# Attention by transposed scores in a fused convolution, attention and step-network kernel

## The reference

```
x = x + depthwise_conv_51x51(group_norm(x))
t = tokens(x)                                # (16, 256, 32)
h = layer_norm(t)
t = t + softmax(mask(Q K^T / sqrt(32))) V Wo + bo   # mask: window, stride, spikes of a sequential gate
h = layer_norm(t)
for p in 33 steps:                           # step network
    op = argmax(h[0, 0, :19])
    if attn_mask[p][op]: h = softmax(h wq wk^T h^T / sqrt(32)) h wv wo
    if ffn_mask[p][op]:  h = relu(h w1 + b1) w2 + b2
t = t + h
```

## Time and profile before

| | us |
|---|---|
| median of 3 runs | 200.5 (199.66 to 201.96) |
| span of the profiled execution | 199.1 |
| TensorE busy | 166.5 |
| VectorE busy | 134.3 |
| ScalarE busy | 111.3 |
| GpSimd busy | 64.1 |

### The profile page before, as it was taken

One profiled execution on the slowest core, in us unless ns is written; L12 is line 12 of the kernel. 1 busy time (PEld: TensorE's weight loads), 2 busy tenths in 40 slices (PEclk: granted clock), 3 DMA queues, 4 the chain that ended last, 5 costly groups with the idle time before them and its releaser, 6 DMA issues.

```text
span 199.1 us, 4262 instructions
## 1 busy us (share of the span) xinstructions
PE 166.5 (84%) x1255; PEld 112.6 (57%) x1256; DVE 134.3 (67%) x382; ACT 111.3 (56%) x324; POOL 64.1 (32%) x153
## 2 busy tenths in 40 slices
PE   7999989693898998879929679999867699998770
PEld 5779744241685776647412468776533587775320
DVE  1364578819938889896506388898756689789481
ACT  3464511429767656555405568675655877664670
POOL 8940000100061555453600005655510036556300
PEclk9999999969579999999966999999999999999997
DMA  5900000000000000000000100000000000000003
GB/s 158 315 3 0 3 0 3 0 3 2 0 2 0 2 0 3 0 0 18 3 7 2 20 0 0 0 0 0 0 0 15 0 0 0 0 0 0 0 0 110
DMA packets 3020, 3.33 MB, mean 17 GB/s; under 512 B 889, under 2 KB 2361, under 8 KB 3002
## 3 DMA queue, kind: packets, MB, share of 16 engines
q1 hardware_dynamic: 2858, 2.85, 4.8%
q10 hardware_dynamic: 144, 0.25, 0.4%
HBM read 2.58 MB, written 0.53 MB: 16 GB/s over the span
## 4 chain that ended last, share of the span: by engine, by line
PE 60%; DVE 16%; issue 9%; ACT 8%; POOL 2%; DVEq 1%; ACTq 1%; POOLq 0%
PE bank L555 17%; PE bank L528 8%; PE bank L615 5%; PE bank L542 5%; ACT qz L981 4%; PE bank L679 4%; PE bank L813 3%; PE bank L512 3%; DVE big L1269 3%; PE bank L633 3%; PE bank L600 2%; POOL prob L448 2%; PE bank L694 2%; ACT qz L1050 1%; ACT prob L905 1%
## 5 line engine op out<-in xcount | busy, mean ns | idle before, releaser
L448 POOL TENSOR_SCALAR prob<-prob,einv 128x256 f32<-128x256 f32 x96 | 44.7, 478 | 60.6 <-DVE einv L1264 60.4
L1269 DVE COPY big<-bank 128x512 f32<-128x512 f32 x48 | 32.9, 685 | 5.7 <-PE bank L528 5.7
L905 ACT ACTIVATE prob<-bank,nmax 128x256 f32<-128x256 f32 x64 | 29.8, 473 | 11.6 <-DVE nmax L1256 11.6
L528 PE MATMUL bank<-ident,prob 128*128 128x128 f32 x192 | 30.2, 280 | 6.5 <-POOL prob L448 6.4
L555 PE MATMUL bank<-hT,qz 128*128 128x256 f32 x128 | 32.7, 383 | 0.0
L528 PEld LDWEIGHTS bank<-ident,prob 128*128 128x128 f32 x192 | 21.4, 140 | 18.2 <-POOL prob L448 14.1
L1256 DVE TENSOR_REDUCE nmax<-bank 128x2 f32<-128x512 f32 x32 | 21.6, 687 | 4.8 <-PE bank L555 4.6
L555 PEld LDWEIGHTS bank<-hT,qz 128*128 128x128 f32 x128 | 22.3, 190 | 3.6 <-issue 1.6
L905 ACT ACTIVATE prob<-minus,nmax 128x256 f32<-128x256 f32 x32 | 16.0, 500 | 8.9 <-DVE nmax L1253 7.9
L555 PE MATMUL bank<-kt,qz 128*128 128x256 f32 x64 | 16.5, 386 | 0.9 <-ACT prob L905 0.9
L905 ACT ACTIVATION_READ_ACCUMULATOR prob<-bank,nmax 128x1 f32 x64 | 12.9, 202 | 0.0
(11 more groups left out here) (173 smaller groups left out, 256.8 us busy)
## 6 DMA issues: line engine op xcount, KB each, us to landing
xrev<-xrev_dram SPq DMA_DIRECT2D x1, 512.0 KB, 4.5
xin<-xtok_dram SPq DMA_DIRECT2D x1, 512.0 KB, 5.0
out_dram<-outT SPq DMA_DIRECT2D x2, 256.0 KB, 3.3
maskc<-maskc_dram SPq DMA_DIRECT2D x1, 256.0 KB, 4.8
kx<-kx_dram ACTq DMA_DIRECT2D x1, 248.0 KB, 3.1
wx<-wx_dram SPq DMA_DIRECT2D x1, 216.0 KB, 2.9
constf<-constf_dram SPq DMA_DIRECT2D x1, 186.0 KB, 4.6
wa<-wa_dram SPq DMA_DIRECT2D x3, 56.0 KB, 1.8
```

What stands on the lines that cost most here:

```text
L448: last = nc.gpsimd.tensor_scalar(prob[b % NPB][:, ih, :], prob[b % NPB][:, ih, :], einv[:, b, ih:ih + 1], 1.0, ALU.mult, ALU.mult)
L528: mm = pe.transpose(bank[2 + b % 2][:, jh * S + ih * P:jh * S + (ih + 1) * P], prob[b % NPB][:, ih, jh * P:(jh + 1) * P], ident)
L905: e = nc.scalar.activation(prob[b % NPB][:, ih, :], scores, ACT.Exp, bias=nmax[:, b, ih:ih + 1], scale=-1.0 if masked else 1.0, accum_out= ...
L1269: nc.vector.tensor_copy(flat(probT[b % NTB]), bank[2 + b % 2][:, :]).then_inc(s_PT, 1)
```

## The change

The product of the attention is turned over. It does the following.

- Queries are drained whole into `qT` (one instruction a group, all on ScalarE), without zeros. `score_pe` multiplies in one row strip of 32 partitions; batch elements 2n and 2n+1 use two strips, and the shifted scores of the pair three rounds earlier use the other two, in turn of h, so that four strips can run side by side.
- The maxima come from these scores (`row_max` as before). GpSimd splits each into three bf16 parts (`parts`, four small instructions for a pair), TensorE turns them to rows (`max_rows_pe`), ScalarE copies the rows to SBUF, and `shift_pe` adds them, by a bf16 product with ones, to every row of a bank; in the masked attention the transposed mask enters by one more bf16 product of 128 rows and 512 columns. `shifted_pe` adds the transposed scores K Q^T onto that.
- ScalarE does one exponential of 512 columns for an element, straight into `probT`. Scaling of `prob`, transposes and `copy_probT` are gone.
- `weigh_pe` also forms the sums of exponentials: a product with ones over `halves`, which GpSimd adds from the two halves of `probT` for elements 0 to 11; for the last group over `probT` itself. `normed_output` on VectorE inverts them (128x256) and multiplies. One bank (6) holds the output of every group.
- The masked attention's residual adds go to GpSimd for groups 0 and 1. A `halves` buffer, the transposed mask (`maskt`, one more load of the size of `maskc`) and a bf16 identity are new. The memset of `qz` on GpSimd is replaced by smaller ones.
- In the loop's body the block of kind 1 stands first, `kind` is computed again, and the attention of the next step follows in the same pass. In the block of kind 3 the products with w2 for groups 0 and 1 are ahead of the second `hidden`. The table load that `nc.scalar.activation(table, Exp)` brings stands once ahead of the loop, not in each attention.

The core of the diff ("..." marks what is left out):

```diff
+        RING = 2
+        NPAIR = B // 2
+        LAG = 3
+        FIRST = 2 * LAG
+        SBANK = [b if b < FIRST else b % 3 for b in range(B)]
+        TBANKS = [3 + b % 3 for b in range(B)]
+        YBANK, MBANK = 6, 7
...
+        ATTY = "DDDD"
+        LPRE = "AAAA" + "AAAA"
...
+        def attention_pool(pool, base, masked):
+            for n in range(NPAIR + 2):
+                if n < NPAIR:
+                    bs = slice(2 * n, 2 * n + 2)
+                    top2 = nmax[:, bs, :].rearrange("p b h -> p h b")
+                    rest2 = rest[:, bs, :].rearrange("p b h -> p h b")
+                    wait(pool, s_nm, base, 2 * n + 2)
+                    nc.gpsimd.tensor_copy(parts[:, :, bs, 0], top2).then_inc(s_hi, 2)
+                    wait(pool, s_hi, base, 2 * n + 2)
+                    nc.gpsimd.tensor_tensor(rest2, top2, parts[:, :, bs, 0], ALU.subtract)
+                    nc.gpsimd.tensor_tensor(parts[:, :, bs, 1], top2, parts[:, :, bs, 0], ALU.subtract).then_inc(s_mid, 2)
+                    wait(pool, s_mid, base, 2 * n + 2)
+                    nc.gpsimd.tensor_tensor(parts[:, :, bs, 2], rest2, parts[:, :, bs, 1], ALU.subtract).then_inc(s_part, 2)
+                if n >= LAG + 1:
+                    for b in (2 * (n - LAG - 1), 2 * (n - LAG - 1) + 1):
+                        if b < B - GB:
+                            wait(pool, s_P, base, b + 1)
+                            nc.gpsimd.tensor_tensor(halves[:, b, :], probT[b][:, 0, :], probT[b][:, 1, :],
+                                                    ALU.add).then_inc(s_ps, 1 if b < B - GB - 1 else 1 + GB)
+                if masked and n >= NPAIR:
+                    masked(n - NPAIR)
...
-        def turn_pe(pe, base, b):
-            wait(pe, s_Pn, base, b + 1)
-            if b >= 2:
-                wait(pe, s_PT, base, b - 1)
-            for jh in range(NH):
-                for ih in range(NH):
-                    mm = pe.transpose(bank[2 + b % 2][:, jh * S + ih * P:jh * S + (ih + 1) * P],
-                                      prob[b % NPB][:, ih, jh * P:(jh + 1) * P], ident)
-            mm.then_inc(s_T, 1)
...
+        def score_pe(pe, b, h, keys):
+            g, rows, at_row = strip(b)
+            mm = pe.matmul(bank[SBANK[b]][:, h * S:(h + 1) * S], qT[rows, g, h * P:(h + 1) * P], keys[rows, g, :],
+                           start=True, stop=True, tile_position=at_row)
+            if h == NH - 1:
+                mm.then_inc(s_S, 1)
+        def shifted_pe(pe, b, h, keys):
+            g, rows, at_row = strip(b)
+            mm = pe.matmul(bank[TBANKS[b]][:, h * S:(h + 1) * S], keys[rows, g, h * P:(h + 1) * P], qT[rows, g, :],
+                           start=False, stop=(h == NH - 1), tile_position=at_row)
+            if h == NH - 1:
+                mm.then_inc(s_T, 1)
...
+        def max_rows_pe(pe, base, n):
+            wait(pe, s_part, base, 2 * n + 2)
+            to = slice(2 * C * (n % 2), 2 * C * (n % 2 + 1))
+            if n >= 2:
+                wait(pe, s_mr, base, 2 * n - 2)
+            for h in range(NH):
+                mm = pe.matmul(bank[MBANK][to, h * P:(h + 1) * P], flat(parts[:, h, 2 * n:2 * n + 2, :]), identb[:, :],
+                               start=True, stop=True, tile_position=(0, 2 * C * (n % 2)))
+            mm.then_inc(s_M, 2)
+        def shift_pe(pe, base, n, masked):
+            wait(pe, s_mr, base, 2 * n + 2)
+            for b in (2 * n, 2 * n + 1):
+                if b >= FIRST - 3:
+                    wait(pe, s_P, base, b - 2)
+                else:
+                    wait(pe, s_nm, base, b + 4)
+                g, rows, at_row = strip(b)
+                if masked:
+                    pe.matmul(bank[TBANKS[b]][:, :], identb[:, :], flat(negmT[:, :, :]), start=True, stop=False)
+                pe.matmul(bank[TBANKS[b]][:, :].rearrange("p (h s) -> p h s", h=NH), onesq[rows, :], rep(mrow[rows, g, :], NH),
+                          start=not masked, stop=False, tile_position=at_row)
...
         def weigh_pe(pe, base, t, k0, g):
+            t.drained(pe, k0 + g)
+            if t is st and g == 0:
+                pe.wait_ge(s_vb, NG * NH)
+            wait(pe, s_P, base, GB * (g + 1))
+            out = bank[YBANK]
             for jh in range(NH):
                 for q in range(GB):
                     b = g * GB + q
+                    pe.matmul(out[q * C:(q + 1) * C, 0:S], v[:, jh, b, :], probT[b][:, jh, :],
+                              start=(jh == 0), stop=(jh == NH - 1), tile_position=(0, q * C))
+            if t is st:
+                pe.matmul(out[:, S:2 * S], onesq[0:1, :], tiny[:, :], start=True, stop=False)
+            if g < NG - 1:
+                wait(pe, s_ps, base, GB * (g + 1) if g < NG - 2 else B)
+                for q in range(GB):
+                    mm = pe.matmul(out[q * C:(q + 1) * C, S:2 * S], onesc[:, :], halves[:, g * GB + q, :],
+                                   start=t is not st, stop=True, tile_position=(0, q * C))
+            else:
+                for jh in range(NH):
+                    for q in range(GB):
+                        mm = pe.matmul(out[q * C:(q + 1) * C, S:2 * S], onesc[:, :], probT[g * GB + q][:, jh, :],
+                                       start=t is not st and jh == 0, stop=(jh == NH - 1), tile_position=(0, q * C))
             mm.then_inc(s_task, 1)
...
+            for h in range(NH):
+                for b in bs:
+                    score_pe(pe, b, h, keys)
+        def attention_pe(pe, base, t, k0, keys, ahead, masked=None):
+            ahead()
+            t.drained(pe, k0)
+            max_rows_pe(pe, base, 0)
+            for n in range(LAG, NPAIR + LAG):
+                if n - LAG + 1 < NPAIR:
+                    max_rows_pe(pe, base, n - LAG + 1)
+                shift_pe(pe, base, n - LAG, masked)
+                if n < NPAIR:
+                    wait(pe, s_nm, base, 2 * n - 1 if n > LAG else 2)
                 for h in range(NH):
+                    for i in range(2):
+                        if n < NPAIR:
+                            score_pe(pe, 2 * n + i, h, keys)
+                    for i in range(2):
+                        shifted_pe(pe, 2 * (n - LAG) + i, h, keys)
+                if n >= LAG + 2 and n % 2 == 1 and n < NPAIR + LAG - 1:
+                    weigh_pe(pe, base, t, k0, (n - LAG - 2) // 2)
+                if masked and n == NPAIR + 1:
+                    masked()
...
+                    wait(pe, s_P, att, B - 2)
+                    t.drained(pe, K_HF - 1)
+                    token0(r)
+                    hidden(r, 0)
+                    token0_row()
+                    weigh_pe(pe, att, t, len(LPRE), NG - 1)
+                    k = K_HF + GB + 1
+                    t.drained(pe, k - 1)
+                    outputs(t, k, (0, 1))
+                    t.drained(pe, k)
+                    hidden(r, 1)
                     next_step(pe, b, reg_r, reg_op, reg_code)
-                    for n in range(NG):
-                        if n % 2 == 0:
-                            t.drained(pe, k0 + GB if n == 0 else k1 + GB)
-                        for q in range(GB):
-                            mm = pe.matmul(bank[ZBANK[n]][q * C:(q + 1) * C, 0:S], w2s, relu[:, q, n, :],
-                                           start=True, stop=True, tile_position=(0, q * C))
-                        mm.then_inc(s_task, 1)
+                    t.drained(pe, k + 2 + GB)
+                    outputs(t, k + 2 + GB, (2, 3))
...
+            copy_rows(0)
+            for n in range(NPAIR):
+                if n + 1 < NPAIR:
+                    copy_rows(n + 1)
+                for b in (2 * n, 2 * n + 1):
+                    wait(act, s_T, base, b + 1)
+                    nc.scalar.activation(flat(probT[b]), bank[TBANKS[b]][:, :], ACT.Exp).then_inc(s_P, 1)
...
+            def normed_output(t, k, g, to):
+                t.filled(dve, k)
+                link(nc.vector.reciprocal(sinv[:, g, :], bank[YBANK][:, S:2 * S]))
+                return nc.vector.tensor_tensor(to[:, g, :], bank[YBANK][:, 0:S], sinv[:, g, :], ALU.mult)
...
+            def attention_dve(base, masked, output, late=None):
+                for b in range(B):
                     row_max(base, b, masked)
+                    if b == B - 3:
+                        output(0)
+                    if late and b >= B - 2 - GB and b < B - 2:
+                        late(b - (B - 2 - GB))
+                output(1)
```

More of the change, by code:

```diff
@@ new lines, in hidden, with outputs @@
+                def hidden(r, gp):
+                    for q in range(GB):
+                        rows = slice(q * C, (q + 1) * C)
+                        if (gp, q) == (1, GB - 1):
+                            pe.wait_ge(s_rowc, r)
+                        pe.matmul(bank[HBANK[gp][q]][:, :], w1r[rows, :], flat(hT[rows, 2 * gp:2 * gp + 2, :]),
+                                  start=True, stop=True, tile_position=(q * C, 0)).then_inc(s_task, 1)
```

(44 more changed lines are left out.)

519 lines of the change are left out of this document (224 added, 295 removed).

## The result

The changed kernel takes 238.2 us (median of 4 runs, 236.3 to 243.0) against 201.1 beside it (199.7 to 202.0): ratio 1.182, interval 1.172 to 1.192. The direction was right, the size was not: 37 us longer where the forecast had 23, and 2 us outside its range. The profiled execution is the slowest of the four, 243.0 us with a span of 241.2; the others had spans of 234.5 to 236.8, so its stages together are 2 to 3% long.

The account below looks back on a forecast made before the run. TensorE, busy 84% of the span, was taken as the bound. 199.1 + 13.0 (masked attention) + 15.6 (two steps) - 4.8 (loop's order) = 222.9 us of span, 224 with 1.4 between span and median; range 203 to 236.

Parts of the forecast that it names:

- The wait for the adds: Plain attention, before the first sums: TensorE waits 4.3 us from the end of round 5's scores for GpSimd's adds.
- the walk: Plain attention followed step by step from its first query product: 36.2 us against 33.3, 2.9 longer.
- The FFN behind it: From 36.2 us to the next query product at 49.0, against 41.2 before: 7.8 longer a step, 15.6 for two.
- table load: Behind the attention's last exponential, ahead of the FFN: a ScalarE load of 1.28 us now on the path.
- The masked attention: From the spikes' end to the last normed group: 55.2 us with the clock against 42.2, longer by 13.0.
- The loop's order: Kind-1 block directly behind its branch: the 3.4 us stop mostly goes, with half-clock FFN and pass time, - 4.8.
- The rival of a stop that stays: Loop, before the first FFN: the stop remains, giving 229, inside the main range; no separate chance given.
- a rival of 9 us at 0.17: Clock falls in TensorE's waits, 2 to 4 us more in each attention: 233 (228 to 238), chance 0.17.
- its 2 us for the clock: Start of the masked attention: TensorE's transposes, spares and scores at the lower clock, + 2.0 us.
- Full drains: Rival, all attentions: each change of tile shape costs 0.41, not 0.17; 21 us more, 245; chance 0.03.
- The cheap helpers: Rival: switches, parts, halves, reciprocal and rounds all at their cheap ends; 208 (201 to 214), chance 0.17.
- the faster case: Rival: rounds at streaming rate, `weigh_pe` never waits, attention walks about 28 us; 192 (187 to 197), chance 0.13.

Follow-up runs that it names:

- with the adds first: Changed kernel with GpSimd adding the halves ahead of splitting the maxima into parts in each turn: 204.4 us.
- the kernel with all spares: Changed kernel, order kept, with spare TensorE products in the waits for the adds, the spikes' wait, layer norm and FFN gaps: 219.7 us, ratio 1.096.
- spares for the spikes: Changed kernel with 56 spare products of 512 columns on TensorE ahead of the wait for the spikes: 243.0 us.
- spares in the waits alone: Changed kernel with 28 spare bf16 products of 256 columns in TensorE's waits for the adds of groups 0 and 1: 222.1 us, ratio 1.094.

## Why the prediction was wrong, step by step

*The wait for the adds* was right in mechanism and size: forecast 4.3 us from the end of the scores, measured 4.4; reciprocal 1.6 forecast, 1.75 measured; halves 0.71 and 0.72; parts 0.9 and 1.0; rounds 2.2 forecast, 2.0 to 2.1 measured. In the attention with its clock held up (125.01 on), the first sums end at 18.3 us (forecast 18.7), the second at 28.4 (29.4). Behind them the walk was too dear: rounds 8 to 10 take 5.0 us, not 6.8, so `hidden` stands at 33.3, not 36.2. Nothing in it asks for more than 0.17 for a change of shape.

*The FFN behind it*: 12.8 us forecast, 12.5 in that run. But one term was wrong: there is no table load. The first relu follows the last exponential at once:

```profile
171.99 1.09 ACT L1025 ACTIVATE big<-bank 128x512 f32<-128x512 f32 x2 [4.11 <-PE bank L581]
172.96 0.27 ACT L1157 ACTIVATE h<-bank,wfs 128x1 f32<-128x1 f32 x1
```

With the table loaded once ahead of the loop, exponentials and relus share it: the changed trace has no load behind 119.84. The Trainium skill, "ScalarE: Activation LUTs", Table sets, says that cheap functions, relu among them, are in every table set beside its one expensive function; by that rule, the changed trace agrees, and the forecast should have left the load out. The kernel before, which names Exp anew in each attention, had one at the exponentials and one at the relus of both its kind-3 steps (112.77 and 144.05 in the first), so where the program puts the load counts too. The 1.28 us is made up for by the way from the second `hidden` to the next query product, 5.6 us where I had 4.9, and by the exponentials, which with the adds first end 2.1 us behind the first `hidden` and not 1.5.

*The masked attention*: +13.0 forecast; +15.9 with the clock mostly held up (58.1 us at a clock of 0.88), +24.3 as it is. I had put 2.0 us on the half clock at its start; it stayed low for 16 us from 56.4 and fell again behind both waits, and a round took 4.2 us (68.08 to 72.29), not 3.1. At full clock a masked round takes 2.4, here in the kernel with all spares, whose spikes end at 58.84:

```profile
82.14 0.64 PE L634 MATMUL bank<-halves,onesc 128*32 128x256 f32 x8
...
93.70 0.30 PE L593 MATMUL bank<-identb,parts 128*64 128x128 bf16 x2
...
96.07 0.30 PE L593 MATMUL bank<-identb,parts 128*64 128x128 bf16 x2
```

Its first sums end 23.9 us behind the spikes, where the walk had 18.8; from there to the last normed group are 34.1 us, where it had 34.4. So what the masked attention took beyond the forecast there lies ahead of the first sums, where the clock was low.

*The loop's order*: -4.8 forecast for the stage. Measured -4.7 alone, and -3.5 in the changed kernel, whose FFN of kind 1 ran at the lower clock. The rival of a stop that stays is out.

*The step that failed* is the clock. The sum ran every product of the three attentions at full clock but for 2 us, and the clock in the waits stood beside it as a rival of 9 us at 0.17. It was no rival but part of the likeliest case: the walk itself had TensorE at work 6 of 15 us, and the trace of before showed the clock fall behind a stretch of 3.34 in 7. The result, 238.2, is just outside that rival's 228 to 238, whose upper end the range had left out. Held up by spares, the clock gives 18.5 us back, twice the rival's price: a low stretch lasts on into the rounds behind it, where TensorE is the bound again, and the three attentions have two such waits each. The sixteen records of products with `v` show it at either level: 1.07 us at full clock (group 0, 145.54), 1.93 below (group 2, 166.93).

*Luck.* Without its 2 us for the clock the forecast is 222, and the kernel with all spares takes 219.7; that they are so close is partly luck. By stages this kernel's trace has 4.9 us more in the masked attention than the walk without those 2 us, of which the low clock ahead of its first sums is the likely reason, and 7.2 less in the two steps, whose walk was too dear.

*The other rivals.* Full drains are out: rounds of 2.0 us hold three changes of shape. The cheap helpers were not cheap (reciprocal, parts and adds are at or above the values taken), yet the faster case's condition, some 28 us for an attention, is met at 27.8 once the adds stand first, with the reciprocal at its full 1.75 us. So what counted was not the helpers' prices, as that rival had it, but their order. It asked for 23.8 us from three attentions; with the adds first the two plain ones give 5.5 and 2.8, and the masked stage is 6.9 longer, so the kernel stays level. The rival's sum was off too: 27.5 us for each walk is 8.7 less, 26 us for three, and 224 less 26 is 198, not 192, unless the masked one comes down further, which the prediction does not work out.

## What to carry to other kernels

Where the trace of before shows the clock fall behind thin stretches, price an idle wait of TensorE at its length and once more for what the engine does behind it: here six waits of 17.2 us took another 17 of clock with them. When two streams share a helper engine, read its program in order and ask for each instruction which one ahead of it waits for something that the waiting engine has yet to release; moving one block may be worth more than making anything cheaper. Where a wait can't be removed, small spare products into a free bank tell within one run about how much of its price is the clock; count their columns, for at twice the meant length they overran the wait by 5.9 us here.

## What the runs showed of the hardware

- In the changed kernel the granted clock went from 1.00 to 0.50 eight times from the wait for the spikes on, seven of them in or up to 1.5 us behind a single wait of TensorE of 2.1 to 6.4 us, and stayed there for 3.3 to 23.5 us, with TensorE busy 15.0 of 15.6 and 10.8 of 11.1 us in two of these stretches; with spares in the same waits the attention ran at 1.00 for 33.3 us.
- It fell without such a wait too: behind 6.2 us of work in 7.7, no wait above 0.9 (spares for the spikes). And a wait of 1.8 us for the output of group 0 had it at 0.50 with spares in the waits alone (products with `v` at 148.48, 1.93 us) and at 1.00 with spares in all gaps (at 148.43, 1.07 us): the same wait does not always bring it down.
- VectorE's reciprocal of 128x256 took 1747 ns, 6.8 ns an element, against 424 ns for the multiply of the same size, 4.1 times: more than the 5.5 that elements 2 to 32 had given.
- Relu and exponential needed no table load between them in the loop, though the kernel before had one at that place; between 98 and 105 us its trace also shows three transfers on instruction queues around a stop of 3.4 us in which no engine worked, and none with the far jump gone.
